# Local attention on one NeuronCore: scores as two 64x64 quarters of the array, and another order inside a chunk

## The reference

```python
def attn_layer(x, Wqkv, qs, ksc, Wo):            # 16 heads of 64
    q, k, v = jnp.split(x @ Wqkv, 3, -1)
    q = l2norm(q) * qs; k = l2norm(k) * ksc
    q = q * cos * scale + rotate_half(q) * sin * scale
    k = k * cos * inv + rotate_half(k) * sin * inv
    out = local_attention(q, k, v)               # windows of 32, each sees itself and the one before
    return out.transpose(0, 2, 1, 3).reshape(b, n, INNER) @ Wo
...
for i in range(DEPTH):                           # 6
    x = attn_layer(shift_tokens(x), Wqkv[i], q_scale[i], k_scale[i], Wo[i]) + x
    x = ffn_layer(shift_tokens(x), ...) + x
```

## Time and profile before

| | |
|---|---|
| median of 3 runs | 5855.41 us (5852.81 to 5869.03) |
| profiled execution, span | 5852.0 us |
| TensorE busy | 5077.2 us, 87% |
| VectorE busy | 4411.0 us, 75% |
| ScalarE busy | 3883.6 us, 66% |
| GpSimd busy | 2947.4 us, 50% |
| mean granted TensorE clock | 0.959 of full |

### The profile page before, as it was taken

One profiled execution on the slowest core, in us unless ns is written; L12 is line 12 of the kernel. 1 busy time (PEld: TensorE's weight loads), 2 busy tenths in 40 slices (PEclk: granted clock), 3 DMA queues, 4 the chain that ended last, 5 costly groups with the idle time before them and its releaser, 6 DMA issues. The chain is left out here.

```text
span 5852.0 us, 136065 instructions
## 1 busy us (share of the span) xinstructions
PE 5077.2 (87%) x38884; PEld 3412.5 (58%) x38884; DVE 4411.0 (75%) x8097; ACT 3883.6 (66%) x12160; POOL 2947.4 (50%) x2878
## 2 busy tenths in 40 slices
PE   5999996998988989889899558989889899898897
PEld 2333332666666666666666446666666666666665
DVE  7888884886867868768688447868868688687785
ACT  2777775775767757767577207757767577577674
POOL 3000002665656656656566216656656566566564
PEclk7999998999999999999999869999999999999999
DMA  0000002122222122221221211122221221212213
GB/s 12 1 2 1 2 1 64 47 60 57 53 68 49 47 71 52 58 60 49 69 52 48 68 52 47 47 73 51 58 60 47 71 52 48 70 47 65 58 47 85
DMA packets 332301, 288.32 MB, mean 49 GB/s; under 512 B 149102, under 2 KB 290708, under 8 KB 329748
## 3 DMA queue, kind: packets, MB, share of 16 engines
q1 hardware_dynamic: 331028, 282.33, 18.8%
q10 hardware_dynamic: 768, 0.02, 0.0%
HBM read 100.81 MB, written 30.41 MB: 22 GB/s over the span
## 5 line engine op out<-in xcount | busy, mean ns | idle before, releaser
L424 DVE TENSOR_REDUCE a_maxima<-a_max 128x1 f32<-128x512 f32 x1024 | 651.6, 686 | 147.0 <-PE a_max L538 141.2
L992 ACT ACTIVATE f_ex<-f_bank,f_nmx 128x96 f32<-128x96 f32 x1536 | 502.8, 339 | 341.8 <-DVE f_nmx L1074 341.6
L992 ACT ACTIVATE g_ex<-g_bank,g_nmx 128x96 f32<-128x96 f32 x1536 | 502.9, 339 | 341.3 <-DVE g_nmx L1074 340.4
L927 POOL TENSOR_TENSOR f_rn<-f_sg,f_minus_half 128x8 f32<-128x8 f32 x384 | 640.6, 1668 | 31.9
L927 POOL TENSOR_TENSOR g_rn<-g_sg,g_minus_half 128x8 f32<-128x8 f32 x384 | 640.1, 1667 | 31.9
L348 ACT ACTIVATE a_pex<-a_scores 128x512 f32<-128x512 f32 x1024 | 531.6, 606 | 157.7 <-PE a_scores L547 157.7
L932 POOL TENSOR_TENSOR f_qr<-f_t 128x512 f32<-128x512 f32 x384 | 549.8, 1432 | 14.7 <-DVE f_t L1093 13.1
L932 POOL TENSOR_TENSOR g_qr<-g_t 128x512 f32<-128x512 f32 x384 | 540.2, 1407 | 14.7 <-DVE g_t L1093 13.1
L1169 PE MATMUL g_bank<-g_wqkv,g_xT 128*128 128x512 f32 x768 | 428.0, 640 | 86.0 <-DVE g_qh L1084 61.5
L1169 PE MATMUL f_bank<-f_wqkv,f_xT 128*128 128x512 f32 x768 | 425.2, 636 | 86.4 <-DVE f_qh L1084 61.4
L1068 DVE TENSOR_TENSOR g_pn<-g_ex,g_rd 128x384 f32<-128x384 f32 x384 | 419.3, 1092 | 13.1
(11 more groups left out here) (242 smaller groups left out, 13216.5 us busy)
## 6 DMA issues: line engine op xcount, KB each, us to landing
f_vw<-f_vt SPq DMA_DIRECT2D x96, 384.0 KB, 4.3
g_vw<-g_vt SPq DMA_DIRECT2D x96, 384.0 KB, 4.3
f_vw<-f_vt SPq DMA_DIRECT2D x96, 256.0 KB, 3.6
g_vw<-g_vt SPq DMA_DIRECT2D x96, 256.0 KB, 3.6
f_vw<-f_vt SPq DMA_DIRECT2D x96, 128.0 KB, 2.3
g_vw<-g_vt SPq DMA_DIRECT2D x96, 128.0 KB, 2.3
f_wqkv<-in_f_Wqkv_dram SPq DMA_DIRECT2D x7, 1536.0 KB, 9.5
g_wqkv<-in_f_Wqkv_dram SPq DMA_DIRECT2D x7, 1536.0 KB, 7.8
```

Of the source, the lines that this page charges most:

```text
L424: dve.tensor_reduce(maxima[:, m // 4, m % 4:m % 4 + 1], ps_max[m % 3][:], AX.X, ALU.max).then_inc(dv_max, 1)
L927: pool.tensor_tensor(rn[:, b, :], sg[:, b, :], minus_half[:], ALU.pow).then_inc(pl_rn, 1)
L992: last = act.activation(ex[:, b, u, :], ps_s[:, KEYS * u:KEYS * u + KEYS], ACT.Exp, bias=nmx[:, b, u:u + 1], accum_out=sm[:, b, u:u + 1])
```

## The change

The query copy keeps its transposed layout (`qT`) with no zeros, and the scores of each head are a product of their own, with 64 rows and 64 columns of the array: the first head in the upper left quarter, the second in the lower right. The memset of `qbd` goes, and with it one count of the semaphore `zeroed`.

```diff
-                            for h in range(2):
-                                r = slice(64 * h, 64 * h + 64)
-                                last = act.copy(qbd[r, pairs, :, 64 * h:64 * h + 64],
-                                                ps_qkT[r, :].rearrange("p (j b q) -> p j b q", j=4, b=2))
-                            last.then_inc(act_qk, 1)
+                            act.copy(qT[:, pairs, :], ps_qkT[:].rearrange("p (j q) -> p j q", j=4)).then_inc(act_qk, 1)
...
-                            last = pe.matmul(ps_s[:, KEYS * u:KEYS * u + KEYS], qbd[:, j, blk, :], kT[:, j, BLK * blk:BLK * blk + KEYS],
-                                             start=False, stop=(u == 3))
+                            for h in range(2):
+                                r = slice(DH * h, DH * h + DH)
+                                last = pe.matmul(ps_s[r, KEYS * u:KEYS * u + KEYS], qT[r, j, BLK * blk:BLK * blk + BLK],
+                                                 kT[r, j, BLK * blk:BLK * blk + KEYS], start=False, stop=(u == 3),
+                                                 tile_position=(DH * h, DH * h))
```

More of the change, by code:

```diff
@@ L688, in local_stack @@
         qr = sb("qr", [P, 2, 512])
-        qbd = sb("qbd", [P, PAIRS, 2, 2 * BLK])
+        qT = sb("qT", [P, PAIRS, P])
         kT = sb("kT", [P, PAIRS, WINDOW + P])
@@ L902, in _ @@
             pool.memset(minus_half[:], -0.5).then_inc(zeroed, 1)
-            for buf in (qbd, kT):
-                pool.memset(buf[:], 0.0).then_inc(zeroed, 1)
+            pool.memset(kT[:], 0.0).then_inc(zeroed, 1)
             def fold_rope(n, kind):
@@ L983, in tile @@
                         act.activation(sq[:, b, :], ps_qk[b][:], ACT.Square).then_inc(act_sq, 1)
[L984 to L987, removed]
+                    if c == 1 and real(t + 1, 0, 0):
+                        put_xT(L, t + 1, 1 - q)
+                    if c % 2 == 0 and real(t, c, 0):
+                        half = c // 2
+                        act.wait_ge(pe_v, upto(pe_v, L, 2 * t + half))
+                        act.wait_ge(ld_vw[1 - q], upto(ld_vw[1 - q], L, (t - 1) >> 1, 48))
+                        act.copy(vt[:, q, 512 * half:512 * half + 512], ps_v[:]).then_inc(act_v, 1)
                     if real(t, c, 4):
@@ L1186, in tile @@
                             j, blk = 2 * g + u // 2, u % 2
-                            last = pe.matmul(ps_s[:, KEYS * u:KEYS * u + KEYS], qbd[:, j, blk, :], kT[:, j, BLK * blk:BLK * blk + KEYS],
-                                             start=False, stop=(u == 3))
-                        last.then_inc(pe_s, 1)
[L1190 to L1195, removed]
+                            for h in range(2):
[3 more added lines that the diff above has]
+                                                 tile_position=(DH * h, DH * h))
+                        last.then_inc(pe_s, 1)
+                    if c == 1 and real(t + 1, 0, 0):
+                        transpose_x(L, t + 1, 1 - q)
+                    if c % 2 == 0 and real(t, c, 0):
+                        half = c // 2
+                        pe.wait_ge(act_v, upto(act_v, L, 2 * t + half - 1))
+                        if half and real(t + 1, 0, 0):
+                            pe.wait_ge(act_xT, upto(act_xT, L, t + 1))
+                        at = 2 * INNER + 512 * half
+                        pe.matmul(ps_v[:], xT[:, q, :], wqkv[:, at:at + 512], start=True, stop=True).then_inc(pe_v, 1)
+                    if c == 3 and real(t - 2, 0, 0):
+                        pe.wait_ge(act_aT, upto(act_aT, L, 4 * t - 5))
+                        pe.wait_ge(dv_y, upto(dv_y, L, t - 3))
+                        for j in range(PAIRS):
+                            last = pe.matmul(ps_y[:, 0:P], aT[:, q, j, :], wo[:, j, :], start=(j == 0), stop=(j == PAIRS - 1))
+                        last.then_inc(pe_Wo, 1)
                     if real(t, c, 7):
@@ L1212, in tile @@
                         last.then_inc(pe_o, 1)
[L1213 to L1221, removed]
-                    if c == 3 and real(t - 2, 0, 0):
-                        pe.wait_ge(act_aT, upto(act_aT, L, 4 * t - 5))
-                        pe.wait_ge(dv_y, upto(dv_y, L, t - 3))
-                        for j in range(PAIRS):
-                            last = pe.matmul(ps_y[:, 0:P], aT[:, q, j, :], wo[:, j, :], start=(j == 0), stop=(j == PAIRS - 1))
-                        last.then_inc(pe_Wo, 1)
+                    if real(t, c, 2):
+                        pe.wait_ge(pl_qr, upto(pl_qr, L, n - 2))
+                        pe.wait_ge(act_qk, upto(act_qk, L, n - 3))
+                        for j in range(4):
+                            last = pe.transpose(ps_qkT[:, P * j:P * j + P], qr[:, b, P * j:P * j + P], ident[:])
+                        last.then_inc(pe_qkT, 1)
             def group(L, m, q):
```

47 lines of the change are left out of this document (22 added, 25 removed).

## The result

The changed kernel took 5619.16 us (median of 4 runs, 5609.39 to 5621.31), the kernel before on the same chip 5857.28 us (4 runs): a ratio of 0.9587, 95% interval 0.9576 to 0.9599. The forecast was 5555 us in a range from 5430 to 5770. The profiled executions span 5852.0 us before and 5618.7 us after, 233.3 us less, where the prediction's sum had 302.

What follows compares the result with a forecast made beforehand. Waits on a chain through TensorE, VectorE and GpSimd were taken as the bound. Steady tile 20.2 to 18.4 us, 1.8 saved over 168 tiles, 302 us: 5855 to 5555 us, range 5430 to 5770.

Steps and rivals of the forecast that it cites:

- The bound: Local attention: waits on one chain, projection, scores, maximum, sum of squares, qh, next projection, 4.47 us a chunk.
- Price of the quarters and switches: TensorE: eight score pairs 0.67 us against 0.87, extra switches 0.3, +0.1 a chunk; tile without waits 18.2 us.
- ScalarE's order: ScalarE: V copy before exponentials, chain 4.25 in chunks of 4.5 us; one query copy saves 1.1 a tile, worth nothing itself.
- pn and qr no longer meet: VectorE: pn follows sum of squares, so misses qr; 0.56 everywhere, saves 1.1 us in about two chunks of four.
- qr and pn in time: TensorE transposes: qr at 7.3 us, read at 7.7; pn read within 0.1 of its end after the short chunk.
- The tightest chain outside TensorE: VectorE and GpSimd: sum of squares to rn's end 2.87 us, round 4.0 to 4.1 a chunk, wait about 0.3.
- The slack of 0.2 us a tile: Steady tile: 0.2 us added to 18.2 for slacks of 0.1 to 0.3 that will not all hold, giving 18.4.
- (1): Rival, TensorE scores: quarters run one after another, 1.33 us, tile 20.9, 5973 us; 6%.
- (3): Rival, TensorE: switches into quarters cost nothing more and nothing waits, tile 17.3 to 17.6, 5370 to 5450 us; 7%.
- (4): Rival, ScalarE: V copy ahead of exp makes a chain as long as that removed, tile 20.2, 5855 us; 4%.
- (5): Rival: GpSimd's qr shuts VectorE out, holding off qh by 1.27 us, tile 21.3, 6040 us; 4%.
- (2): Rival: new wait of about 0.25 us a chunk, rn before qh or exp behind V copy; tile 19.3, 5704; 18%.

Runs made afterwards that it cites:

- the kernel with V in chunk 1: Changed kernel with second half of the V projection in chunk 1, transpose of x in chunk 2, V copy behind key copy: 5545.3 us, ratio 0.9464.
- the kernel with the values behind the scores: On the kernel with V in chunk 1: values product directly behind scores, both V copies behind query or key copy; 5511.41 us, ratio 0.9387.

## Why the prediction was right, and where its size was off

- **The bound.** Right that waits set the tile and not TensorE's work: quarters without the order gave 0.999, the order without quarters 0.9647. The one chain behind them is only in part shown. In chunk 0, by whose rows I worked it out, it cost the next projection nothing: the V projection, from 1610.93 and 0.96 long, ends with `qh`, at 1611.88. What it did set is the root behind the sum of squares, and `qr` behind the root, and so the 0.32 us wait. In chunk 1, ahead of the 0.47 us wait for `qh`, the maximum doesn't wait for the scores. It stands behind a long `pn`. In the kernel before:

```profile
1613.43 1.27 POOL L932 TENSOR_TENSOR f_qr<-f_t 128x512 f32<-128x512 f32 x1
1613.62 1.50 DVE L1068 TENSOR_TENSOR f_pn<-f_ex,f_rd 128x384 f32<-128x384 f32 x1
1615.04 0.55 DVE L1074 TENSOR_REDUCE f_nmx<-f_bank 128x4 f32<-128x384 f32 x1
```

By the distances of chunk 0 (projection to scores 1.46, scores to maximum 1.21; the step at L1169 is 0.1 longer here) the scores would have let it start at 1614.6 to 1614.7. So the meeting of `pn` and `qr`, which I had named as an extra "on top", makes 0.3 to 0.4 us of that wait, an estimate from these rows. VectorE's order put back cost some 130 us (0.9806 against 0.9587) and brings both back, so it doesn't divide them.
- **Price of the quarters and switches.** Right. Forecast 18.2 us a tile without waits; the kernel with V in chunk 1, whose TensorE has none, shows 18.23. From the first score record to the next full product I had 0.67 + 0.05 + 0.09 = 0.81 (0.79 in the line on ScalarE's order, a slip), and 0.81 it is.
- **pn and qr no longer meet.** Right: `pn` is at 0.56 in every chunk.
- **qr and pn in time.** Right in steady tiles. Behind the short chunk it is as close as I had it: `pn` ends at 1513.05, and the weights of its transposes are loaded from 1513.10.
- **The tightest chain outside TensorE.** Wrong in size. I had 2.87 us from the sum of squares to the end of `rn`, as in the earlier trace rows, and a round of 4.05 us with 0.3 of wait. With `sg` and `rn` begun under VectorE's two-input work the round is 4.59 us (sum of squares to the end of `rn` 3.48, from 2.87 + 0.34 + 0.27; then `qh` and maximum) and the wait 0.95 in three chunks of four. Three such rounds and one of 4.18 with the residual sum are 17.95, as the kernel with the values behind the scores shows, under the tile of 18.54. So in steady tiles it cost nothing, as the clamp's removal shows; at the start of a layer it did.
- **ScalarE's order.** The V copy ahead of the exponentials fitted, as worked out, and bought nothing (0.9563 against 0.9587). The single query copy I had called worth nothing by itself; it and the quarters together bring some 30 us, and the rows put the gain on the copy.
- **The slack of 0.2 us a tile.** The figure was near, its source missed. The step that I left out is the key copy, which stands behind the exponentials on ScalarE and which chunk 2's mask needs: 0.31 us a tile. I had priced the chain for the V chunks (4.25 of 4.5) and not for the short chunk 1, where exponentials and two key copies make 4.03 against 3.73.
- **Where the missing 69 us are** (302 forecast, 233.3 between the profiled executions). The sum was 25.2 us a layer over 14 tiles. The twelve phases together shrank by 254.3 us, 21.2 a layer. Of the 4.0 that are missing in a layer some 2.3 are steady tiles, which gave 1.7 and at the end of a layer 1.4 instead of 1.8 (18.54 and not 18.4; the last two of before are 19.9, not 20.2). The other 1.7 are the start, which I had at zero for two tiles and at 1.8 for the third: the first gained 0.75, the second lost 1.3 (16.93 to 18.26, medians), the third gained 0.7 (20.28 to 19.56). The second is VectorE's and GpSimd's round: there is no residual sum in it yet, and four rounds of 4.5 to 4.6 us are 18.3, more than the tile took before. Without the clamp it is 16.0. So filling does not keep its length when a chain becomes longer.
- **Outside the phases** 21.0 us were given back. Of these 3.8 lie ahead of the first layer (991.11 to 994.90 us) and 8.8 from the last projection of the first stack to the first of the second (288.9 to 297.7 us), most of them in the linear attention, which the change doesn't touch. The granted clock of that stretch was 0.73 before and 0.71 after, and the 32 records of L1577 (L1575 after) took 696 and 851 ns on average. The kernel with the quarters alone, whose phases are nearly as long as before, has 298.0 us there, and the kernels of this study range from 287.8 to 299.0. So these 12.6 us differ from execution to execution and say little of the change. The remaining 8.4 stand behind the other phases, 0.8 us each; what makes them no run showed.

The rivals: (1) and (3) are out by the records, (4) and (5) by the timeline: the steady tile's only wait before a mask is for the key copy, and `qh` took 0.69 (from 1510.42) under a `qr` begun at 1510.36, so GpSimd didn't hold VectorE off. Of (2) a third came true, 0.31 us a tile from one missed slack in place of 0.25 a chunk.

## What to carry to other kernels

When a chain of waits is broken, work out the next chain for every chunk of the cycle, and first for the shortest one: what was slack in the long chunks was 0.3 us too little in the short one. The start of a pipeline has a cycle of its own, too: a round that is free in steady tiles cost 1.3 us in the second tile of every layer. Moving an engine's step in front of work that another waits for is only free while its own input comes early; the same ScalarE order gave 0.96 with one TensorE order and 1.06 with another. And an edit to the busiest engine can pay on another one: the quarters made TensorE's chunk 0.12 us longer and still brought some 30 us, by the copy that they spare ScalarE.

## What the runs showed of the hardware

- Two products in diagonal quarters run at once although they write one PSUM bank, on different partitions: single records start 0.007 and 0.076 us apart in turn, eight pairs of records of 96 f32 columns at 0.083 a pair (0.13 for the first). The Trainium skill (TensorEngine Tiling (Array Packing), Gotcha 1: PSUM Pressure) says that different row tiles can't access one bank simultaneously. This trace does not agree.
- The order of issue decides the overlap: alternating quarters 0.81 us, one quarter after the other 1.18.
- GpSimd's small instructions become longer when they start under a VectorE instruction with two inputs in SBUF. The clamp of 128x8 elements otherwise takes 0.24 us; begun under `pn` it takes 0.58 and ends 0.10 us after `pn`, in all 276 cases of the first stack. The root otherwise takes 1.67 us; begun under `t1` it takes 1.94, begun under `pn` 1.88, and in all 378 cases it ends 1.52 or 1.53 us after the end of that instruction. So only the first 0.15 us or so of the root (1.67 - 1.52) is held up, an estimate from these figures. The Trainium skill (SBUF — State Buffer, SBUF: two separate sides) holds that of a VectorE instruction with two SBUF inputs and a GpSimd instruction that reads SBUF the one that starts first has the shared port pair for its whole instruction. The clamp agrees, and so does the start of the root. The rest of the root does not: `t1`, begun 0.20 us after it in the earlier trace rows, ran at 0.69.
